# The second attention's softmax maxima: the pass that finds them set half a round ahead, and the maxima carried as three contraction rows copied by DMA

## What is computed

```python
q = (x @ wq).reshape(B, T, 16, 8)
lat = x @ w_down                       # width 64
k = (lat @ wk_up).reshape(B, T, 16, 8)
v = (lat @ wv_up).reshape(B, T, 16, 8)
q, k = rope(q), rope(k)
scores = einsum('bqhd,bkhd->bhqk', q, k) / sqrt(8)
allowed = page(key) <= page(query)     # pages of 32 tokens
attn = softmax(where(allowed, scores, min))
x = x + einsum('bhqk,bkhd->bqhd', attn, v).reshape(B, T, 128) @ wo
```

## Time and profile before

| | |
|---|---|
| median of three runs | 499.72 us (498.47 to 499.89) |
| profiled execution | 502.12 us, its span 500.1 us |
| busy, share of the span | PE 419.6 us (84%), DVE 314.2 (63%), ACT 232.1 (46%), POOL 214.2 (43%) |
| mean granted TensorE clock | 0.905 of full speed |
| second attention, rounds -1 to 8 | about 245 to 415 us |

### The profile page before, as it was taken

The page is one execution under the profiler, slowest core; times in us unless marked ns, Lnnn a source line. Parts: engine busy times, 40 slices in busy tenths (PEclk is TensorE's granted clock), DMA queues, the critical chain, the costliest instruction groups (busy, mean ns, idle before and its releaser), DMA issues.

```text
span 500.1 us, 15672 instructions
## 1 busy us (share of the span) xinstructions
PE 419.6 (84%) x5250; PEld 326.9 (65%) x5251; DVE 314.2 (63%) x1173; ACT 232.1 (46%) x565; POOL 214.2 (43%) x312
## 2 busy tenths in 40 slices
PE   8898899998657999986758989989888788799980
PEld 8676588776446999964536556655555566698980
DVE  4765578888744555449576568568876536454543
ACT  2667556666402555301235656756655420255540
POOL 5433335555531344524554635643722433134440
PEclk9989999998757999988788999999998767799996
DMA  8999700000001122130000000000000000111216
GB/s 233 304 242 345 217 3 15 12 11 11 13 17 32 55 65 63 42 90 1 2 2 1 1 1 3 0 0 0 1 2 13 23 17 26 33 49 57 61 47 178
DMA packets 44339, 28.60 MB, mean 57 GB/s; under 512 B 7200, under 2 KB 40480, under 8 KB 44288
## 3 DMA queue, kind: packets, MB, share of 16 engines
q1 hardware_dynamic: 38096, 20.83, 15.0%
q0 software_dynamic: 2496, 5.13, 2.8%
q10 hardware_dynamic: 3696, 1.97, 1.4%
HBM read 12.76 MB, written 15.16 MB: 56 GB/s over the span
## 4 chain that ended last, share of the span: by engine, by line
PE 58%; DVE 16%; issue 9%; DMA 6%; ACT 5%; DVEq 3%; POOL 2%; SPq 1%; another core or an unknown queue 0%; POOLq 0%; ACTq 0%
PE S L1436 7%; PE bank L1446 6%; PE S L1344 6%; PE bank L1303 5%; PE bank L1320 3%; PE bank L1559 3%; DVE nm L757 2%; PE bank L1476 2%; PE S L1276 2%; PE bank L1330 2%; PE bank L1249 2%; PE S L1530 2%; PE bank L1570 2%; PE S L1529 2%; ACT E L1012 2%
## 5 line engine op out<-in xcount | busy, mean ns | idle before, releaser
L916 ACT ACTIVATE E<-S,nmax 128x256 f32<-128x256 f32 x128 | 58.9, 474 | 45.5 <-DVE nmax L541 41.1
L1149 POOL DMA_INDIRECT slots<-yo,token x46 | 44.1, 958 | 73.5 <-DVE yo L697 54.7
L1012 ACT ACTIVATE E<-S 128x1536 f32<-128x1536 f32 x32 | 46.4, 1450 | 24.9 <-PE S L1535 24.8
L1108 POOL TENSOR_TENSOR vs<-Va,rden 128x512 f32<-128x512 f32 x32 | 33.3, 1039 | 57.0 <-DVE rden L576 49.5
L1436 PE MATMUL S<-xgT,W1s 128*128 128x128 f32 x368 | 51.9, 285 | 1.5 <-DVE xgT L683 1.3
L1446 PE MATMUL bank<-W,hT 128*128 x368 | 49.7, 279 | 0.2
L1436 PEld LDWEIGHTS S<-xgT,W1s 128*128 128x128 f32 x368 | 45.3, 194 | 4.5 <-issue 2.1
L973 ACT ACTIVATE hT<-S,b 128x128 f32<-128x128 f32 x92 | 28.7, 363 | 41.8 <-PE S L1436 39.8
L757 DVE TENSOR_REDUCE nm<-bank 128x2 f32<-128x512 f32 x64 | 41.0, 682 | 8.2 <-PE bank L1502 8.1
L1446 PEld LDWEIGHTS bank<-W,hT 128*128 128x128 f32 x368 | 45.6, 195 | 0.5 <-issue 0.5
L541 DVE TENSOR_REDUCE nmax<-S 128x4 f32<-128x1024 f32 x32 | 39.0, 1219 | 10.2 <-PE S L1344 9.4
(11 more groups left out here) (181 smaller groups left out, 984.3 us busy)
## 6 DMA issues: line engine op xcount, KB each, us to landing
rows<-zeros SPq DMA_DIRECT2D x1, 8768.0 KB, 30.8
xg<-rows SPq DMA_DIRECT2D x46, 64.5 KB
W<-in_L_ffn_W SPq DMA_DIRECT2D x1, 2048.0 KB, 10.0
x<-in_L_attn_a_x SPq DMA_DIRECT2D x4, 256.0 KB, 5.7
yg<-slots SPq DMA_DIRECT2D x8, 128.0 KB, 3.5
yg<-slots ACTq DMA_DIRECT2D x8, 128.0 KB, 3.7
slots<-yo,token POOLq DMA_INDIRECT x46
yg<-in_select SPq DMA_DIRECT2D x1, 512.0 KB, 7.8
```

Source lines behind the costliest of these rows:

```text
L916: last = act.activation(E[:, hp, h, c, :], S[hp % 2][:, h, c * T:(c + 1) * T], ACT.Exp, bias=nmax[:, hp, k:k + 1], accum_out=den[:, hp, k: ...
L1012: act.activation(Eb[:, q % 2, :, :], S4[:, 0:3, :], ACT.Exp, scale=SCALE_B).then_inc(bs["exp"], 1)
L1108: pool.tensor_tensor(vs[:, q, :, :, :], v, r, ALU.mult).then_inc(a_vs, 1)
L1149: pool.indirect_dma_start(out=y_dram, out_offset=bass.IndirectOffsetOnAxis(token[:, turn_at, :], 0), in_=yo[:, turn_at % 2, :], in_offset=None
```

## The change

1. **Order.** The maximum pass of a batch is spread over two rounds: steps 0 and 1 of batch b+2 stand late in round b, steps 2 and 3 of batch b+1 early in round b. The half transposes that they need, and their copies, move with them. A round -2 is added ahead. The projection `b_kv` is now done at the start of round b for batch b+2 (it was at the end of round b-1, for the same batch), and with it `b_turn_k`; `b_split`, `b_repeat` and the first half transposes of that batch come behind it in the same round.
2. **Banks.** From batch 2 on, q and k are projected into `pb[3]`, the latent and v into `pb[2]`, which also take the maximum pass. So `b_q` and `b_kv` wait for a `b_max`, and `b_kv` is four products of 128 columns instead of two of 256.
3. **Maxima.** The constant of k has ones in three of its eight zero rows. `mT` has 48 rows (half, part, head pair), and SP copies it with six DMAs for each batch (1 partition x 8 x 256 bfloat16, 4 KB each) into the three rows of `qT` in each half. The 16 `sel` products of 256 columns and 16 of 128 for each batch are gone. `b_scoresT(b, 0)` waits for the six DMAs (`mrow`) instead of `mT`. `in_select` is now the masks, 32 KB.
4. The router's steps are set at other points; step 2 of round 6 ends in round 7. Copies of k's halves change engines (ACT i = 0, DVE i = 1).

The diff, cut:

```diff
@@ b_rounds @@
-            for b in (-1, 0):
+            for b in (-2, -1, 0):
@@ sync @@
+            def b_maxima_rows():
+                for b in range(B):
+                    sp.wait_ge(bs["mT"], b + 1)
+                    for h in range(2):
+                        for k in range(3):
+                            r, j = 64 * h + 56 + k, (3 * h + k) * 8
+                            sp.dma_start(qT[r:r + 1, b % 2, :, :], mT[j:j + 8, :]).then_inc(bs["mrow"], 16)
@@ vector, b_round @@
...
+                if m and since(b, 0): b_turn_k(b + 2)
                 if n: b_kT(b + 1, 1 - p)
...
                 if l: b_normal(b - 1, 0)
...
-                if n: b_max(b + 1, 0)
-                if n: b_max(b + 1, 1)
...
+                if n: b_max(b + 1, 2)
                 if l: b_normal(b - 1, 1)
...
-                if n: b_max(b + 1, 2)
-                if nn: b_repeat(b + 2, p)
-                if nnn: b_turn_q(b + 3)
+                if m and since(b, -1): b_repeat(b + 2, p)
+                if n: b_max(b + 1, 3)
...
                 if l:
                     dve.wait_ge(bs["at"], b)
...
-                if n: b_max(b + 1, 3)
-                if nnn: b_turn_k(b + 3)
+                if there(b + 3) and since(b, -1): b_turn_q(b + 3)
+                if m: b_max(b + 2, 0)
...
                     dve.tensor_tensor(xs, xs, pb[1][:, 0:T].rearrange("p (u c) -> p u c", u=2), ALU.add
...
+                if m: b_max(b + 2, 1)
@@ scalar, b_round @@
...
-                if n: b_kT(b + 1, 1 - p)
                 if c: b_exp(b, 2)
...
+                if there(b + 3) and since(b, -1): b_latent(b + 3)
+                if m: b_kT(b + 2, p)
                 if c: b_outT(b, p, 1)
...
                 if n:
                     act.wait_ge(bs["mt"], b + 2)
+                    waits(act, bs["mrow"], (b + 1) * 96)
+                    act.copy(mT[:, :], pb[2][0:48, 0:P].bitcast(BF16)).then_inc(bs["mT"], 1)
@@ gpsimd, b_round @@
...
+                if there(b + 2) and since(b, -1):
+                    b_split(b + 2, p)
...
                 if there(b + 1):
+                    b_maxima(b + 1)
                     b_place_v(b + 1, 1 - p)
@@ tensor @@
...
             def b_kv(b):
                 pe.wait_ge(bs["latT"], b + 1)
...
+                else:
+                    pe.wait_ge(bs["max"], ((b - 1) * 4 + 1) * 3 + 2)
+                    for i, bank in enumerate(proj(b)):
+                        for u in range(2):
+                            last = pe.matmul(bank[:, u * D:(u + 1) * D], latT[:, u * P:(u + 1) * P],
+                                             wkv[:, i * D:(i + 1) * D], start=True, stop=True)
...
             def b_scoresT(b, p, q):
...
                 if q == 0:
-                    pe.wait_ge(bs["mT"], b + 1)
+                    pe.wait_ge(bs["mrow"], (b + 1) * 96)
...
+                early(0, 0)
+                late(0, 1)
+                late(1, 1).then_inc(bs["low"], 1)
+                early(1, 0)
+                early(0, 1)
+                early(1, 1)
+                pe.wait_ge(bs["low"], b * 4 + q + 1)
+                late(0, 0)
+                last = late(1, 0)
                 last.then_inc(bs["st"], 1)
@@ tensor, b_round: the new order (router steps left out) @@
...
+                if n: b_tq(b + 1, 1 - p, 1)
+                if m and since(b, 1): b_kv(b + 2)
...
+                    b_values(b - 1, 1 - p, 3)
...
+                if c: b_scoresT(b, p, 0)
...
+                if n: b_tk(b + 1, 1 - p, 1)
+                if l: b_natural(b - 1, 1 - p, 0)
...
+                    b_scores(b + 1, 1 - p, 2)
+                if c: b_scoresT(b, p, 1)
...
                     b_natural(b - 1, 1 - p, 1)
+                if n: b_scores(b + 1, 1 - p, 3)
...
+                    b_values(b, p, 0)
...
+                if m: b_tq(b + 2, p, 0)
+                if c: b_scoresT(b, p, 2)
...
+                if there(b + 3) and since(b, -1): b_q(b + 3, 1 - p)
+                if m: b_tk(b + 2, p, 0)
...
+                    b_scores(b + 2, p, 0)
...
+                if c: b_scoresT(b, p, 3)
...
+                if m and not at(b, -1): b_scores(b + 2, p, 1)
...
                     b_values(b, p, 2)
```

More of the change, by code:

```diff
@@ L292, in b_rounds, with since, at, proj @@
                 round_(b, b % 2)
-        def router_at(b, point):
-            return {(5, 0): 1, (6, 0): 2, (7, 0): 3, (7, 1): 4, (7, 2): 5, (7, 3): 6, (8, 0): 7}.get(
-                (b, point) if isinstance(b, int) else None)
+        def since(b, first):
+            return not isinstance(b, int) or b >= first
+        def at(b, *rounds):
+            return isinstance(b, int) and b in rounds
+        def proj(b):
+            early = isinstance(b, int) and b < 2
+            return (pb[0], pb[0]) if early else (pb[3], pb[2])
         def b_parts(eng, chain, p, k):
@@ L788, in b_round @@
             def b_round(b, p):
-                n, nn, nnn, l = there(b + 1), there(b + 2), there(b + 3), there(b - 1)
-                if isinstance(b, int) and b == 5:
+                n, m, c, l = there(b + 1), there(b + 2), there(b), there(b - 1)
+                if at(b, 5):
                     dve.wait_ge(bs["x"], 4)
[L792 to L795, removed]
+                    for k in range(2):
+                        norm_stats(3, k, k)
@@ L836, in b_round @@
                                       ).then_inc(bs["x"], 1)
-                if isinstance(b, int) and b >= 7:
+                if at(b, 7, 8):
                     dve.wait_ge(bs["x"], b)
                     norm_stats(3, b - 1, (b - 1) % 2)
[L840 to L848, removed]
+                if m: b_max(b + 2, 1)
+                if at(b, 7):
+                    router_first(1, 6)
+                    router_second(1, 6)
+                if at(b, 8):
+                    router_second(1, 7)
+                if at(b, 5, 6):
+                    for k in ((1, 2) if b == 5 else (3,)):
+                        norm_apply(3, k, k % 2)
+                if at(b, 6):
+                    router_first(1, 2)
             chain0 = Chain(dve, bs["chain0"])
@@ L1532, in late @@
-                def late(d, h, add):
-                    n, dst = 2 * q + d, S4[:, 2, (2 * d + h) * P:(2 * d + h + 1) * P]
-                    if add:
-                        return pe.matmul(dst, sel[rows[h], n, :], mT[rows[h], 1, :], start=False, stop=True)
-                    return pe.matmul(dst, kT[rows[h], p, n, P:T], qT[rows[h], p, n, P:T], start=True, stop=False)
-                for d in range(2):
-                    early(d, 0, False)
-                    late(d, 1, False)
-                    last = late(d, 1, True)
-                    early(d, 0, True)
@@ L1543, in b_scoresT, with early @@
-                last.then_inc(bs["low"], 1)
-                for d in range(2):
-                    early(d, 1, False)
-                    if d == 0:
-                        pe.wait_ge(bs["low"], b * 4 + q + 1)
-                    late(d, 0, False)
-                    early(d, 1, True)
-                    last = late(d, 0, True)
+                def early(d, h):
+                    n = 2 * q + d
+                    return pe.matmul(S4[:, h, d * T:(d + 1) * T], kT[rows[h], p, n, 0:P], qT[rows[h], p, n, :],
+                                     start=True, stop=True)
@@ L1672, in router_second @@
                     ranks(1, h - 2, pb[3])
-            def b_router(b, point, rounds, what):
-                if isinstance(b, int) and b in rounds:
-                    what(router_at(b, point))
             pe.wait_ge(b_loaded, 80)
```

282 lines of the change are left out of this document (134 added, 148 removed).

## The result

The changed kernel takes **525.4 us** (median of 4 runs, 523.7 to 525.9) against 499.8 of the kernel before on the same chip: ratio 1.049, 95% interval 1.043 to 1.055. Slower, as forecast; the time is 10 us above the 515 of the prediction and inside the range of 500 to 529. The profiled execution has a span of 522.9 us against 500.1, 22.8 more.

A forecast was written before the change was run, and what follows sets the result against it. PE bounded the rounds before; the new loop through POOL's split was to bind after. Start +12, rounds 1 to 5 +7.3, rounds 6 and 7 -7.3, clock +3 make +15: median 515 us, range 500 to 529.

The forecast's parts named there:

- The loop: Steady rounds: kv, turn of k, split, repeat, transposes and maxima close in 18.9 us in place of 17.43, error some 0.7.
- The rival that PE stays the bound: Rounds fall toward PE's 15.6 us if the loop is 3 us shorter; 491 us, 484 to 498, chance 0.14.
- The clock: Rounds: PE's 2.4 us idle lowers the clock, some 3 us where it falls; one such round taken, +3.
- The rival (nearly every round: The clock falls in nearly every round, 3 us each time: 530 us, from 524 up; chance 0.20.
- the main case: The loop binds the rounds and the clock costs one round's 3 us: 515 us, 505 to 524, chance 0.52.
- Rounds 1 to 5: Five steady rounds, each 18.9 us in place of 17.43: +7.3.
- The start: Up to round 1: late mT(0), six DMAs, the loop and 1.2 of half clock put round 1 at 291, +12.
- Rounds 6 and 7: Last rounds: 13.8 for round 6 plus 21.2 for round 7 in place of 42.32, so -7.3.
- The split's 6.65 us: POOL's split in each steady round keeps its length of 6.65 us beside DVE's work.
- The rows by DMA: Six DMAs per batch take 4.4 to 5 us, covered in steady rounds, exposed in round 0, about 1.5 in round 7.
- The small costs: PE's steps in a round: scoresT 0.45 us (0.35 to 0.55), kv 1.28; PE's work from 16.2 to about 14.2.
- The part ahead: First attention and mixtures, counted as the rest: no change, 1 us either way.

The follow-up runs named there:

- e3: The kernel after, with six idle matmuls in PE's wait ahead of the transposes of q in each round from round 0; 522.6 us, ratio 1.044.
- e1: The kernel after, with GpSimd's split cut in two and its q half run half a round earlier; 507.3 us, ratio 1.010 against the kernel before.
- e8: e7 with pairs of idle matmuls added in PE's waits of rounds -2 to 0; 500.1 us, ratio 1.002 against the kernel before.
- e7: e1 with scores(1, 1) and kv(2) ahead of scoresT(0, 0) in round 0, and two DMAs of three partitions for six of one; 504.1 us.
- e9: e8 with two more groups of three idle matmuls in PE's waits of round 0; 499.5 us, ratio 1.013 against the kernel before.
- e10: e9 with eight more idle matmuls at the end of round 6 and in round 7's first steps; 499.1 us, ratio 1.010 against the kernel before.

## Why the prediction was right, step by step

- **The loop.** Right in its mechanism and nearly in its size. The turn of k was priced from a row of the turn of q (326.10), which has the same six instructions; it took 1.01 us where 0.93 was planned. Against the plan in us from kv: turn done 2.4 (2.2 measured), PE's wait 2.4 (2.44) until 9.93 (10.1), `b_q` done 12.48 (13.7), transposes of k done 13.04 (14.7), `scores(b+2, 0)` 15.0 (16.5), next kv 18.9 (20.5). Up to the wait everything fits; then come the doubled times of `b_q` and the transposes, which the step had at the full clock. At the full clock it is 19.3 at most (e3), inside the 0.7 that I gave. The rival that PE stays the bound needed a loop of 17.4; e1 shows that it comes true as soon as 3.1 us of split are out.
- **The clock.** Mis-sized twice, in opposite directions. I had it fall in one round of six at 3 us; it fell in each of rounds 1 to 5 (0.92 in the first four, 0.82 in the fifth; 1.00 in round 6), in the first four at 1.35. In these four that makes 5.4 us in place of 3; in round 5 its price isn't known. The rival (nearly every round, from 524 us up, chance 0.20) had the right frequency, and at its price of 3 us would have given 530. The measured 525.4 lies 1.4 us above the main case's own 505 to 524 and within this rival: its condition came true, at less than half its price.
- **Rounds 1 to 5**: +7.3 and the clock's +3 were forecast, +14.1 came.
- **The start, mis-sized: +17.0 in place of +12.** From the first transposes, `mT(0)` took 19.8 us where the step had 16.5, the rows 5.5 where it had 5, and from `kv(2)` to round 1 it was 22.7 where it had 21. Ahead of the wait for the rows I costed the serial passes of batches 0 and 1 at the clock that they had before, which was full until 258 us; it was half over the whole 38 us from 246 on. How much of the 5 us is the clock's is known only in part: e8's idle matmuls, with the clock between 0.76 and 1.00 until 264 us, took 2.7 us off this stretch in e7's version; e9's further ones, with the clock at 1.00 from 256 to 280 us, took off no more. PE's timeline and the window:

```profile
265.24 0.39 PE L1560 MATMUL S<-QT,keys 64*128 64x256 bf16 x1 [3.44 <-DMA QT<-mT]
268.00 2.04 PE L1500 MATMUL bank<-wkv,latT 64*128 64x128 f32 x8 [1.09 <-DVE nm L776]
```

```profile
246.00:284.00 38.00, 26.14 (x183) 16.83 (x186) 18.70 (x49) 11.27 (x14) 12.47 (x25) 0.50 0.01 2
```

The forecast wait of 4 us ahead of the first `scoresT`, ended by a DMA, is the first row. `kv(2)` at 2.04 us is twice what a kv takes in a round.
- **Rounds 6 and 7: -3.8 in place of -7.3.** Round 6 was right (13.8 forecast, 14.3 measured). Round 7 was not: 24.2 in place of 21.2. I took the saving of four `scoresT` off a round whose clock I left as it was; that the clock is what ate it is argued from the windows, and no run tried it apart. Windows of round 7 after, and of before:

```profile
412.00:416.00 4.00, 4.00 (x30) 2.83 (x29) 3.51 (x25) 1.13 (x2) 2.19 (x3) 0.50 0.12 37
424.00:428.00 4.00, 4.00 (x33) 2.36 (x31) 2.54 (x15) 1.84 (x3) 2.83 (x4) 0.50 0.10 33
```

```profile
390.00:394.00 4.00, 2.59 (x40) 1.53 (x39) 2.48 (x17) 2.19 (x3) 2.90 (x4) 1.00 0.12 37
```

After, the clock is 0.50 from about 411 us to the round's end; before, it was back at 1.00 for 4 us in the middle.
- **The split's 6.65 us**: 6.65 again (333.41 to 340.06). The Trainium skill ("GPSIMD Engine Reference", Key points) puts GpSimd's contention with DVE on instructions in a 2-port mode or with two SBUF inputs. Between 333.41 and 340.06 DVE ran one copy, the reductions and `b_normal`, all out of PSUM and with at most one input from SBUF, and the trace agrees: the split is as long as before.
- **The rows by DMA.** Hidden in steady rounds, as forecast; in round 7 they cost 0.22 us, not 1.5. The term's parts were a little low: six issues took 4.29 us on SP's queue, 0.7 each, where the earlier trace rows gave 0.43. The section of the Trainium skill that I named there tells of DMAs that GpSimd issues; the 2.2 us that the term rests on is a row of SP's own queue.

```profile
259.77 4.29 SPq L418 DMA_DIRECT2D QT<-mT  x6
```

- **The small costs.** `scoresT` takes 0.57, 0.57 and 0.48 us (0.45 forecast, 0.55 the bound), kv 1.1 (1.28). PE's work was to fall from 16.2 to 14.2 us a round; at the full clock it is 14.84 (e1), so a third of that saving didn't come. In the closed loop this cost nothing.
- **One sign was wrong**: PE's busy time was to fall by 15 us and rose by 7.5. With 232 matmuls fewer I put that down to the lower clock (0.863 in the mean against 0.905); how much each stretch adds was not worked out.
- **The part ahead** was put at 0 ±1; it differed by -5.5, and by up to 8 us between executions of kernels alike up to there. That ±1 was too sure. It hid a part of the loss: the parts behind it are 28 us longer together, where +15 was forecast. Without it the time would be near 528 us, an estimate from the table, 1 us below the upper end of the range. So that the time came out this near to 515 is in part luck.

## What to carry to other kernels

Work that is prepared a round ahead is slack for every engine on its way: before pulling a step half a round closer to its use, write the whole chain from it back to itself with all engines on it, and compare its length with the round, not with the busy time of the fullest engine. When such a loop has closed, look for the part of its longest step whose input is there earlier (here the half of q) rather than for a faster engine. And a wait of PE inside a loop may have to be priced with a longer time of the steps behind it: here 1.35 us for a wait of 2.44.

## What the runs showed of the hardware that I had not expected

- **The clock fell to half (1.2 of 2.4 GHz) behind a wait of 2.44 us, round for round**; in e1's rounds, whose waits are 0.2 to 0.7 us, it stayed full. The fall came late: the first transposes and `scoresT` after the wait ran at full speed (0.62 and 0.57 us), and the 4 us after them at 0.56 and 0.59.
- **In round 7 it stayed at 0.50 with PE busy 4.00 of 4.00 us**, in two windows (412 to 416, 424 to 428 us). Why is open; e10's idle matmuls ahead of it put the fall off by some 7 us and didn't shorten the run.
- **A small DMA's issue cost 0.7 us on SP's queue from SBUF to SBUF, out of eight partitions into one** (4.29 us for six of 4 KB), and 0.88 out of 24 partitions into three with 12 KB (1.75 for two, in e7): so here fewer, larger ones carried the same bytes in 40% of the issue time. The Trainium skill ("DMA: Bandwidth & Descriptors", Anatomy of one DMA) gives a fixed cost for each DMA that GpSimd issues; these are SP's, and here the part that adds up from one to the next was 0.7 us.

```profile
259.71 1.75 SPq L418 DMA_DIRECT2D QT<-mT  x2
```
